# Spreading a layer norm over twelve written-out attention steps, moving the MLP bias products to the last pairs, and reordering the two mask programs

## What is computed

```python
xn = layer_norm(x, norm1_g, norm1_b)            # rolled by 4, cut in 64 windows of 64 tokens
q, k, v = split(xn @ qkv_w.T + qkv_b)           # 16 heads of 8
q, k = rope2d(q), rope2d(k)
attn = softmax(q * 8**-0.5 @ k.T + attn_mask)
x = x + roll_back((attn @ v) @ proj_w.T + proj_b)
a, gate = split(layer_norm(x, norm2_g, norm2_b) @ fc1_w.T + fc1_b)
x = x + (silu(gate) * a) @ fc2_w.T + fc2_b
f, g, h = x @ Wq + bq, x @ Wk + bk, x @ Wv + bv # each of 4 images, 1024 tokens
out = gamma * softmax(f @ g.T) @ h + x
```

## Time and profile before

| | us |
|---|---|
| median of 3 runs | 410.89 |
| the runs | 407.49, 411.99, 410.89 |
| the profiled execution, its own time | 412.08 |
| span of that execution in the profile | 410.2 |
| layer-norm and pair stage, first to last L1083 | 27.59 to 189.70 |

### The profile page before, as it was taken

One profiled execution on the slowest core, in us unless ns is written; L12 is line 12 of the kernel. 1 busy time (PEld: TensorE's weight loads), 2 busy tenths in 40 slices (PEclk: granted clock), 3 DMA queues, 4 the chain that ended last, 5 costly groups with the idle time before them and its releaser, 6 DMA issues.

```text
span 410.2 us, 12175 instructions
## 1 busy us (share of the span) xinstructions
PE 365.2 (89%) x4732; PEld 230.1 (56%) x4732; DVE 302.5 (74%) x831; ACT 272.8 (67%) x436; POOL 259.2 (63%) x313
## 2 busy tenths in 40 slices
PE   2687899989999999998789999999989999989793
PEld 0454555656566656565445445544556766757573
DVE  8776678888888888889737667687558787885524
ACT  2768587777778887787825644445577867768481
POOL 6656467676777777698676755654236765768421
PEclk9998889999999999999989999999999999999889
DMA  6611011110100011110000000000001011010101
GB/s 178 232 26 29 8 27 32 27 32 23 33 25 27 26 27 28 30 28 15 2 2 1 14 13 2 2 0 1 15 13 27 2 53 27 2 54 2 53 1 53
DMA packets 15594, 12.19 MB, mean 30 GB/s; under 512 B 3991, under 2 KB 14136, under 8 KB 15544
## 3 DMA queue, kind: packets, MB, share of 16 engines
q1 hardware_dynamic: 14304, 11.03, 9.3%
q10 hardware_dynamic: 1240, 0.48, 0.5%
HBM read 4.15 MB, written 2.10 MB: 15 GB/s over the span
## 4 chain that ended last, share of the span: by engine, by line
PE 58%; DVE 19%; ACT 5%; DMA 5%; issue 5%; POOL 4%; SPq 3%; DVEq 0%; POOLq 0%; ACTq 0%
PE ps L346 8%; PE ps L1565 7%; PE ps L866 6%; DMA k_t<-qk_t 5%; PE ps L894 4%; PE ps L952 3%; PE ps L887 3%; PE ps L875 3%; PE ps L360 3%; PE ps L856 3%; SPq L825 3%; PE ps L1400 3%; DVE ob L1688 2%; DVE mx L1657 2%; PE ps L858 2%
## 5 line engine op out<-in xcount | busy, mean ns | idle before, releaser
L1739 POOL TENSOR_TENSOR el<-e,eh 128x1024 f16<-128x1024 f32 x28 | 59.6, 2130 | 42.8 <-ACT eh L1731 42.5
L1274 POOL TENSOR_TENSOR p_lo<-e_buf,p_hi 128x1024 f16<-128x1024 f32 x32 | 68.2, 2131 | 5.6 <-ACT p_hi L1127 3.6
L1266 POOL TENSOR_TENSOR rot<-ta,tb 128x256 f32<-128x256 f32 x32 | 23.3, 728 | 42.4 <-DVE tb L1051 42.2
L346 PE MATMUL ps<-y_t,fc_w 128*128 128x512 f16 x192 | 46.2, 381 | 3.7 <-POOL al L272 2.5
L866 PE MATMUL ps<-mask,identb 128*128 128x512 bf16 x128 | 40.3, 398 | 8.2 <-DMA k_t<-qk_t 7.5
L1724 ACT ACTIVATE e<-ps 128x1024 f32<-128x1024 f32 x32 | 32.7, 1022 | 21.7 <-PE ps L1554 21.2
L1192 ACT ACTIVATE e_buf<-ps 128x1024 f32<-128x1024 f32 x32 | 32.7, 1023 | 19.9 <-PE ps L887 19.8
L1083 DVE TENSOR_REDUCE ps<-ps 128x16 f32<-128x1024 f32 x32 | 39.4, 1232 | 7.8 <-PE ps L875 7.0
L1565 PE MATMUL ps<-val,eh 128*128 128x129 f16 x512 | 38.6, 226 | 5.8 <-DVE ob L1688 5.1
L1565 PEld LDWEIGHTS ps<-val,eh 128*128 128x128 f16 x512 | 33.0, 100 | 14.6 <-issue 8.8
L287 POOL TENSOR_TENSOR hl<-hid,hh 128x512 f16<-128x512 f32 x24 | 27.6, 1157 | 21.3 <-DVE yn L532 11.3
(11 more groups left out here) (166 smaller groups left out, 980.2 us busy)
## 6 DMA issues: line engine op xcount, KB each, us to landing
k_t<-qk_t SPq DMA_DIRECT2D x128, 32.0 KB, 1.8
x_all<-in_x SPq DMA_DIRECT2D x8, 256.0 KB, 5.0
out<-ob SPq DMA_DIRECT2D x8, 192.0 KB, 2.1
yr<-xr SPq DMA_DIRECT2D x16, 64.0 KB, 2.0
mask_f<-in_mask SPq DMA_DIRECT2D x1, 512.0 KB, 3.6
fc_w<-in_fc_w SPq DMA_DIRECT2D x1, 512.0 KB, 6.2
out<-ob SPq DMA_DIRECT2D x4, 128.0 KB, 1.9
fc_w<-in_fc_w SPq DMA_DIRECT2D x1, 256.0 KB, 5.9
```

The costliest lines, as they stand in the source:

```text
L346: last = pe.matmul(ps[:, bank, :], fc1_w16[:, ws, 128 * block_:128 * block_ + 128], y_t[:, v, ys, :], start=(n == 0), stop=(n == 2))
L1274: pool.tensor_tensor(p_lo[:, u], e_buf[:, u], p_hi[:, u], ALU.subtract).then_inc(plo_done, 1)
L1739: pool.tensor_tensor(el[:, T % H_BUFS, :], e4[:, T % E_BUFS, :], eh[:, T % H_BUFS, :], ALU.subtract).then_inc(el_done, 1)
```

## The change

Six things change together.

1. Layer norm chunks 2 to 7 are turned one at a time, in steps 1, 3, 5, 7, 9 and 11 (`LN_STEP`). All use `T1_BANK`, between two uses of it by `turn`: PE waits for DVE's copy of the keys first (`qt_ready`), and the next step's `turn` waits for the chunk's low half (`ln_ready`). ACT normalises two tiles of a chunk in each of the two steps ahead, POOL's roots go to steps -1 to 3, DVE's statistics to steps -1, 0 and 1. Twelve steps are written out before the loop (12 to 27 in two rounds of eight) and seven behind it.
2. The MLP bias products move from step -1 to step 31 (`left == 3`) on PE, DVE's part too; `turn_a(1, 1)` waits for them.
3. The program of PE is put in two branches of an `If` that hold pairs, MLP and global attention; the one-part program stands first and is reached without a jump, and the three-part copy is jumped over at the end.
4. Start: norm1's gains have a semaphore of their own; DVE no longer clears half of `k_t` and takes chunk 2's statistics later; POOL clears slots 0 and 1 of `k_t` first and 2 and 3 in step -1.
5. Of pair 0's four key DMAs two are started by ACT, beside SP.
6. `turn_x` uses transposes instead of fp32 products.

```diff
-            LOOP_FROM, LOOP_TO = WPAIRS, PAIRS - WPAIRS
-            LN_BANK = (PV_BANK, ST_BANK, ST_BANK + 1, PV_BANK, ST_BANK, PV_BANK, PV_BANK, PV_BANK)
-            LN_BANK_FREE = (0, 0, 0, 1, 2, 4, 6, 7)
+            LOOP_FROM, LOOP_TO = 12, PAIRS - 4
+            LN_BANK = (PV_BANK, ST_BANK) + (T1_BANK,) * (CHUNKS - 2)
+            LN_STEP = {2 * c - 3: c for c in range(2, CHUNKS)}
+            def ln_chunk(n, first=0):
+                return LN_STEP.get(n - first) if isinstance(n, int) else None
...
# PE, body(n)
-                    if isinstance(n, int) and n == 0:
-                        pe.wait_ge(fc1_b_ready, 1)
                     if valid(n, -1):
                         wait(pe, lo_done, n + 2)
                         wait(pe, qt_ready, n + 1)
+                        if ln_chunk(n, 1):
+                            pe.wait_ge(ln_ready, ln_chunk(n, 1) + 1)
                         turn(t1_ps[:, 0], q_rows[:, (r + 1) % BUFS])
...
-                    if at_step(n, 0):
-                        ln_turn(3)
-                        ln_turn(4)
...
+                    if ln_chunk(n):
+                        pe.wait_ge(qt_ready, n + 2)
+                        ln_turn(ln_chunk(n))
...
-                    if isinstance(n, int) and n == -1:
-                        mlp_pe(pe)[2]()
...
# PE, early(left)
+                if left == 3:
+                    bias()
                 if left == 2:
+                    pe.wait_ge(fc1_b_ready, 1)
                     turn_a_waits(1)
...
# DVE
-                for rows in (k_t[:, 0:2], q_rows[:], k_rows[:]):
+                for rows in (k_rows[:], q_rows[:]):
...
+                    if ln_chunk(n):
+                        ln_lo_of(ln_chunk(n))
+                    if at_step(n, 0) or at_step(n, 1):
+                        ln_stats_of(4 + 2 * n)
+                        ln_stats_of(5 + 2 * n)
...
# ACT
+                    if at_step(n, -2):
+                        ln_hi_of(1)
                     if at_step(n, -1):
+                        act.wait_ge(qt_ready, 1)
+                        act.wait_ge(keys_set, 1)
+                        for j in (2, 3):
+                            rows = slice(ROWS * j, ROWS * j + ROWS)
+                            act.dma_start(k_t[rows, 0, j], qk_t[rows, 0, 1]).then_inc(kz_ready[0], 16)
                         act.wait_ge(mask_loaded, 16)
                         copy(mask16[:, 0], mask_f[:]).then_inc(mask_hi, 1)
+                        ln_norm_of(2)
...
+                    if ln_chunk(n):
+                        ln_hi_of(ln_chunk(n))
...
+                    for ahead in (1, 2):
+                        c = ln_chunk(n, -ahead)
+                        if c and c > 3:
+                            ln_norm_of(c, range(2 * (2 - ahead), 2 * (2 - ahead) + 2))
...
# POOL
+                    if isinstance(n, int) and 0 <= n < 4:
+                        ln_rstd_of(4 + n)
...
             def turn_x(b, h):
-                four_tiles(pe, b, h, AUX, ident[:]).then_inc(xt_done, 1)
+                for k in range(4):
+                    last = pe.transpose(ps[:, AUX, 128 * k:128 * k + 128], tokens(b, 512 * h + 128 * k, 128), ident[:])
+                last.then_inc(xt_done, 1)
...
+            with pe.If(rest < 1):
+                other_pairs(1)
+                pe_mlp(pe)
+                pe_last(pe)
+            with pe.If(rest > 0):
+                other_pairs(3)
+                pe_mlp(pe)
+                pe_last(pe)
```

More of the change, by code:

```diff
@@ L132, in build @@
         turn_loaded = sem("turn_loaded")
+        gains_loaded = sem("gains_loaded")
         qkv_loaded = sem("qkv_loaded")
@@ L784, in other_steps @@
                     body(n, n // 2, n % WPAIRS)
-                with eng.Fori(LOOP_FROM // WPAIRS, LOOP_TO // WPAIRS) as it:
-                    for w in range(WPAIRS):
-                        body(it * WPAIRS + w, it * (WPAIRS // 2) + w // 2, w)
+                with eng.Fori(0, (LOOP_TO - LOOP_FROM) // WPAIRS) as it:
+                    for k in range(LOOP_FROM, LOOP_FROM + WPAIRS):
+                        body(it * WPAIRS + k, it * (WPAIRS // 2) + k // 2, k % WPAIRS)
                 for n in range(LOOP_TO, LAST + 1):
@@ L822, in body @@
                         sp.wait_ge(qt_ready, n + 2)
-                        for j in range(4):
+                        if at_step(n, 1):
+                            sp.wait_ge(keys_set, 2)
+                        for j in range(2 if at_step(n, -1) else 4):
                             rows = slice(ROWS * j, ROWS * j + ROWS)
@@ L827, in _, with pe_pairs @@
                 steps(sp, body, nothing)
-            @block.tensor
-            def _(pe):
+            def pe_pairs(pe):
                 def ln_turn(c):
                     pe.wait_ge(ln_norm, c + 1)
-                    wait(pe, ln_ready, LN_BANK_FREE[c])
                     for k in range(TPC):
@@ L1118, in _ @@
                 act.dma_start(ln_const[:], t["ln_const"]).then_inc(ln_loaded, 16)
-                for dst, name in ((g1b1, "g1b1"), (qkv_w, "qkv_w"), (qkv_b, "qkv_b")):
+                act.dma_start(g1b1[:], t["g1b1"]).then_inc(gains_loaded, 16)
+                for dst, name in ((qkv_w, "qkv_w"), (qkv_b, "qkv_b")):
                     act.dma_start(dst[:], t[name]).then_inc(qkv_loaded, 16)
@@ L1133, in ln_hi_of, with ln_norm_of @@
                          ps[:, LN_BANK[c], :].rearrange("p (t q) -> p t q", t=TPC)).then_inc(ln_hi, 1)
-                def ln_norm_of(c):
+                def ln_norm_of(c, tiles=range(TPC)):
                     act.wait_ge(ln_rstd, c + 1)
                     wait(act, ln_turned, c - 3)
-                    for k in range(TPC):
+                    for k in tiles:
                         last = act.activation(xn[:, c % 4, 128 * k:128 * k + 128], x_all[:, TPC * c + k, :],
                                               ACT.Identity, bias=nmr[:, c, k:k + 1], scale=rstd[:, c, k:k + 1])
-                    last.then_inc(ln_norm, 1)
+                    if tiles[-1] == TPC - 1:
+                        last.then_inc(ln_norm, 1)
                 act.wait_ge(v_set, 4)
-                act.wait_ge(rows_set, 4)
+                act.wait_ge(rows_set, 3)
                 act.activation(warm[:], v_hi[:, 0, 0, 0, 0, 0:1], ACT.Exp)
                 act.wait_ge(gains_ready, 1)
+                act.wait_ge(qkv_loaded, 32)
                 act.activation(w_scaled[:, 0:3 * DIM], qkv_w[:], ACT.Identity, bias=0.0, scale=gains[:, 0:1])\
@@ L1235, in _ @@
                 pool.wait_ge(v_set, 4)
-                pool.memset(k_t[:, 2:BUFS].bitcast(F32), 0.0).then_inc(keys_set, 1)
+                pool.memset(k_t[:, 0:2].bitcast(F32), 0.0).then_inc(keys_set, 1)
                 pool.wait_ge(ln_loaded, 16)
@@ L1282, in body @@
                     if at_step(n, -1):
+                        ln_rstd_of(2)
+                        pool.memset(k_t[:, 2:BUFS].bitcast(F32), 0.0).then_inc(keys_set, 1)
                         ln_rstd_of(3)
-                        ln_rstd_of(4)
                         pool.wait_ge(mask_known, 1)
```

97 lines of the change are left out of this document (25 added, 72 removed).

## The result

The changed kernel took 407.21 us (median of 11 runs, 405.90 to 410.58) against 410.10 us for the kernel before (11 runs, 406.52 to 413.66): ratio 0.9938, 95% interval 0.9911 to 0.9964. It is faster, by 0.6%, which is inside the 1% that counts here as no change. Single executions more than 1.5% above the fastest of their kernel are left out of the ratios, and of the medians given for experiments 1 (three of 12), 2 (one of 12, which took 1088 us) and 10 (one of 12). The profiled execution took 408.14 us with a span of 406.3, so 3.9 us less span than before.

The account below looks back on a forecast made before the run. PE was taken to bound the loop, busy for all 4.76 us of a step. Terms -3.1, -1.1, +1.2 and -1.7 sum to -4.7, taking the median 410.89 to 406.2; forecast band 404 to 408.5, 8-in-10 range 400.5 to 412.

Parts of the forecast that it names:

- Start of step 0, -3.1: Opening: without bias products and the jump there, step 0 starts at about 20.6 instead of 23.71, ended by the mask copy.
- about 0.5 of that can be the jump: PE's 1.03 us idle before its first weight load: the jump over the three-part program accounts for about 0.5.
- Steps 0 to 12, -1.1: Step 0's maxima to step 12's: spreading the layer norm chunks takes 68.0 us to 66.9.
- rival A: Steps 0 to 12: the clock comes up early, so they take 63.7 us; total 403, chance 0.24.
- chunk steps of 5.3 beside even ones of 4.8: Steps 3 to 12: steps with a layer norm chunk take 5.3 us, set by PE and ACT; even ones 4.8.
- marks of error: Step 0 after 22, clock under 1.00 in steps 5 to 11, chunk step over 5.8, or last stage no shorter.
- B's chain: Chunk steps: `turn` waits for DVE's low half, DVE's copy follows; 5.9 us instead of 5.3; total 409.7, chance 0.22.
- the clock of C: Chunk steps at PE's lower clock after pauses from 1.3 us on; five take 7.2 us; total about 416, chance 0.12.
- Bias at step 31, +1.2: Before step 31's last turned scores: the moved bias products take about 2 us and delay what follows by 1.2.
- `turn_x`, -1.7: Last stage: transposes save 0.6 us a call, counted for three of eight calls, those on the chain ending last.
- The end, 0: From tile 31's exponential to the end: no change, though PE now jumps over the three-part copy there.
- Up to 6 us are hidden: End of kernel: PE's last products run at 403.11, the span ends at 410.2, so up to 6 us of jump are hidden.

Follow-up runs that it names:

- experiment 1: Changed kernel with MLP and last stage standing once on PE, so its jump falls between the pairs and the MLP: 409.13 us, ratio 0.9951.
- experiment 2: Changed kernel without the three-part copy, so PE has no jump at all: 407.40 us, ratio 0.9930.
- experiment 10: Kernel before the change with only the bias products moved to step 31: 412.80 us, ratio 1.0048.
- experiment 12: Changed kernel with three-part pairs first again, mask copy ahead of the pairs, and bias products ahead of the MLP's first products: 407.51 us, ratio 0.9944.
- experiment 6: Changed kernel with three-part pairs first and jumped over behind step -1, MLP and last stage shared: 408.38 us, ratio 0.9955.
- experiment 9: Changed kernel with bias products back in step -1, `turn_x` as products and three-part pairs first again: 408.75 us, ratio 0.9950.
- experiment 4: Changed kernel with the bias products back in step -1: 410.75 us, ratio 1.0009.
- experiment 7: Changed kernel with ACT's mask copy moved ahead of the pairs, right behind chunk 1's normalisation: 408.58 us, ratio 0.9954.
- experiment 8: Changed kernel with the bias products moved from step 31 to just ahead of the MLP's first products: 407.57 us, ratio 0.9941.
- experiment 5: Changed kernel itself timed again, without edits, against the kernel before: 408.35 us, ratio 0.9970.

## Why the prediction was right or wrong, point by point

The median of 407.2 is 1.0 above the forecast of 406.2 and inside its own band of 404 to 408.5. The likeliest verdict, more than 1% faster (0.52), did not come. The terms did less well.

*Start of step 0, -3.1: measured -3.36, by the chain named.* But the reason why the removed products were worth that is incomplete. The step that failed is "about 0.5 of that can be the jump": the 1.03 us of idle in the earlier trace rows are what the jump left uncovered, not what it costs. It leaves PE idle for 3.0 to 3.8 us where nothing lies beside it (experiments 1, 10, 12), and before the change most of that lay beside the 3.57 us of products. Taking the products alone bared it, and won 0.34. The change wins 3.4 only because its jump is out of the way as well; with the jump back at the start but the wait for the mask behind it, experiment 6 starts as early. Step by step, step 0's maxima go from 27.59 to 26.85 with the shorter opening (experiment 9), to 26.00 without the jump (experiment 4), and to 24.23 with the products gone too. The sum came out since it took products and jump away together.

*Steps 0 to 12, -1.1: measured -1.94, by two errors against each other.* Steps 0 to 2 took 17.04, where 18.4 to 19.6 were forecast. Step 0 ran at the lower level, but from 29.6 on the clock was up and stayed up: rival A's mechanism, without its 63.7 us. Steps 3 to 11 took 90.28 - 41.27 = 49.01 against 47.2. The term "chunk steps of 5.3 beside even ones of 4.8" is mis-sized: by PE's work it is right (5.21 busy), but two steps take 10.8 to 11.2, not 10.1. In steps 7 and 11 ACT's half normalisation reaches PE 0.89 late; I had listed ACT's work as 5.28 and 4.69 and not asked when its last piece comes. The pairs of steps without this wait are as long, though, with waits for keys (1.08 in step 8) and for POOL's rows (0.55 in step 4), so what sets the pair stays open. One of my own marks of error was met: chunk steps 1, 7 and 11 took over 5.8. PE's timeline shows no wait of B's chain (the `turn` behind DVE's low half), and the clock of C did not come in this trace. In that of experiment 7 it did, in steps 8 and 9 (6.75 and 6.22 us), which was another mark of error. Nor do pauses of 1.3 us decide it, as C had it: one of 1.32 at 114.4 in experiment 2 left the clock up, one of 1.30 at 71.8 in experiment 7 stood ahead of its fall at 73.2.

*Bias at step 31, +1.2: products 1.90, stretch +0.71* in this trace. Over all traces the stretch scatters too much to price them: 113.35 to 117.30 in the nine with the products at step 31, 112.70 to 114.05 in the three with them early. One part was not in the sum. In experiment 2 the clock is at its lower level from 189.2 to 192.6, so that the mask products behind the bias take 0.95 instead of 0.59; granted clock 0.96 and 0.87 in 180 to 200. Of the nine traces seven show a clock under 1.00 in 180 to 200, of the three with early products none. But the products can't be the only cause. In experiment 8 the clock fell at 189.4 as well, in the turned scores (0.69 at the higher level), and there the products came only behind it:

```profile
189.23 0.98 PE L894 MATMUL ps<-q_t,k_t 128*64 128x64 f16 x32
...
193.73 1.93 PE L493 MATMUL ps<-g1b,fc_w 128*128 128x1 f32 x16
```

What lets the clock fall there stays open.

*`turn_x`, -1.7: measured -0.74.* The 0.5 for a call is right (1.09 to 0.59), but "three lie on the chain that ends last" is not what counts: seven calls shorten their step, which is 3.5. What was missing is that DVE then leads the next step and 2.0 of it come back, and that the clock is lower behind the longest of these steps. In this trace the clock also falls once more, from 302.7 to 306.1, in the second of the stage's steps (3.77 instead of 2.67); the other traces with transposes, but for experiment 1, have 94.4 to 94.6 for this stretch, those with products 95.1 to 95.8.

*The end, 0: measured +1.07.* "Up to 6 us are hidden" was said of PE's time. It holds for that: no engine waits for PE. But two more packets of instructions come in beside the last output, which then lands later (2.9 instead of 1.8 us), and nothing hides that. That the two share the DMA engines would explain it; no run shows it directly. The Trainium skill ("Runtime: NRT & Kernel Launch", Instruction fetch mechanics) says that a taken branch out of the fetched window stalls until its target is there. The trace agrees, with 3.0 to 3.8 us here and a second price at the output DMA; the prediction had set the rule aside for a row that showed only the remainder.

*What stays open.* The gain of steps 0 to 12 rests on single traces, and those scatter: experiment 10, with the old pile, took 65.10 there, less than the changed kernel, in the fastest of its 12 runs. Nor do the parts add up. By the timed medians the spread alone gives -2.1, the bias move alone +2.0, and yet the changed kernel with the bias taken back (experiment 4) stands at 1.0009, the changed kernel at 0.9938 and 0.9970. The jump explains part: it decides what the products are worth at the start (0.3 in experiment 10, 1.8 in 4). Experiments 4 and 9 differ by `turn_x` and the place of the jump alone, and stand 2.0 apart, the wrong way round for `turn_x`; their traces differ by that much in no stretch. But the trace of 4 is its fastest run, 3.2 us under its median, with a mean clock of 0.986 where its 12 runs have 0.979 (those of 9 have 0.988). So other executions of 4 spend time at the lower level that its one trace lacks. Where, I can't say.

## What to carry to other kernels

A jump over a copy of the program cost PE some 3 us here, and the trace shows only what of it sticks out: before taking away work that stands beside a jump, ask what that work hides. Put the wait behind the jump, not ahead of it, and no output DMA beside it. Work piled into few steps costs more than its own time if the pauses lower the clock; in the one trace that tried it, one piece to a step was enough. Ask also when an engine's last piece comes, not only how busy it is. Profile a typical execution before pricing a part from it: the fastest of 12 runs lay up to 3.4 us under the median. After a removed wait, look for the next arrival (here mask at 20.2, then keys at 21.6) before pricing the gain.

## What the runs showed of the hardware that was not expected

- A taken jump on PE: 3.46 us of idle in the middle (0.63 without), 3.77 behind a wait, 3.01 in experiment 12; nothing to be seen beside a wait of 3.38. From the packet of instructions that it starts to the next matmul it is 3.1 us (experiment 1), 2.7 (10) and 3.0 (12). With its two extra packets beside it a 128 KB output lands in 2.9 us, not 1.8.
- Where the code stands seems to decide which steps are long. In steps 12 to 19 of the changed kernel (5.47, 4.96, 4.76, 5.52, 4.95, 4.76, 4.76, 5.86) the three longest each have a packet on PE's instruction queue and a wait of 0.86 to 0.93 for keys. With the other order of copies (experiment 6) the same steps are 4.76, 4.76, 5.29, 4.95, 4.77, 4.79, 5.34, 5.32. Such packets also fall into three of the steps of 4.76 to 4.96, so it is not the packet alone.
- The granted clock differs between executions of one kernel: the 12 runs of the changed kernel in experiment 5 have means of 0.965 (412.09 us) to 0.985 (406.81 us). The clock is not all of it: one run at 0.981 took 410.86. All 12 span 406.06 to 412.09, which is wider than any part of this change.
